# A three-stage decoder layer on one core: mask bound, weight splits and the self-attention tail moved, and the output projection placed ahead of probabilities-by-values

## The reference, cut to what matters

```python
def _L0_attn_ref(x, Wq, bq, Wk, bk, Wv, bv, Wo, bo):
    q = (x @ Wq.T + bq).reshape(b, l, h, hd).transpose(0, 2, 1, 3)
    k, v = ...
    scores = jnp.einsum('bhqd,bhkd->bhqk', q, k) / math.sqrt(hd)
    att = jax.nn.softmax(jnp.where(causal, scores, -jnp.inf), axis=-1)
    return jnp.einsum('bhqk,bhkd->bhqd', att, v)... @ Wo.T + bo
def _L0_xattn_ref(query, key, value, mask, wq, wk, wv, wo):
    q, k = _rope(q), _rope(k)
    scores = jnp.einsum('bhgqd,bhkd->bhgqk', qg, k) / scale
    masked = jnp.where(mask[:, None, None].astype(bool), scores, -1000000000.0)
    return (softmax(masked) @ v) @ wo
x = _layernorm(x + _L0_attn_ref(x, ...))
x = _layernorm(x + _L0_xattn_ref(x, ctx_4096, ctx_4096, mask, ...))
x = _layernorm(x + _L0_ffn_ref(x, ...))
```

## Time and profile before

| what | before |
|---|---|
| runs | 1770.31, 1770.8 (median), 1776.01 us |
| the profiled execution's own time | 1773.97 us |
| its span, first to last instruction | 1772.2 us |
| mean granted TensorE clock | 0.982 of full speed |
| PE busy | 1695.6 us (96% of the span) |
| DVE, POOL, ACT busy | 1267.5, 964.8, 919.0 us |
| self-attention | from 0 to about 302 us |
| cross-attention | from about 303 us |

### The profile page before, as it was taken

The page is one execution under the profiler, slowest core; times in us unless marked ns, Lnnn a source line. Parts: engine busy times, 40 slices in busy tenths (PEclk is TensorE's granted clock), DMA queues, the critical chain, the costliest instruction groups (busy, mean ns, idle before and its releaser), DMA issues. The chain is left out here.

```text
span 1772.2 us, 39039 instructions
## 1 busy us (share of the span) xinstructions
PE 1695.6 (96%) x15461; PEld 968.1 (55%) x15461; DVE 1267.5 (72%) x2048; ACT 919.0 (52%) x1518; POOL 964.8 (54%) x875
## 2 busy tenths in 40 slices
PE   6899998699999999999999999999889999999997
PEld 4666665365555555555555555555555555455553
DVE  5777776678888888888888888888786444344445
ACT  5776764555546564646464555455742333333334
POOL 5556672745645454646464646464743555455545
PEclk9999999899999999999999999999988999999999
DMA  4522312311312222214131222121166778887658
GB/s 147 146 65 47 85 48 36 117 37 58 110 62 83 83 68 89 97 42 149 37 108 61 72 72 96 37 104 40 61 226 198 153 151 222 221 208 153 115 100 300
DMA packets 88897, 190.68 MB, mean 108 GB/s; under 512 B 14800, under 2 KB 33744, under 8 KB 86672
## 3 DMA queue, kind: packets, MB, share of 16 engines
q1 hardware_dynamic: 65232, 130.72, 22.1%
q0 software_dynamic: 22912, 57.32, 15.8%
q10 hardware_dynamic: 576, 0.14, 0.0%
HBM read 124.95 MB, written 63.21 MB: 106 GB/s over the span
## 5 line engine op out<-in xcount | busy, mean ns | idle before, releaser
L1112 POOL TENSOR_TENSOR xa_sc<-xa_sc,xa_rs 128x1024 f32<-128x1024 f32 x32 | 60.9, 1903 | 374.4 <-DVE xa_rs L1360 374.4
L1099 POOL TENSOR_TENSOR xa_xs<-xa_xs,sn 128x512 f32<-128x512 f32 x160 | 234.1, 1463 | 45.7 <-ACT xa_xs L1153 45.7
L288 PE MATMUL bank<-xhl,front_h 128*128 128x512 f16 x640 | 245.4, 383 | 10.9 <-DVE front_l L648 9.7
L289 PE MATMUL bank<-xhl,front_h 128*128 128x512 f16 x640 | 245.2, 383 | 0.0
L290 PE MATMUL bank<-xhl,front_l 128*128 128x512 f16 x640 | 245.0, 383 | 0.0
L1104 POOL TENSOR_TENSOR xa_rr<-xa_x,xa_xs 128x512 f32<-128x512 f32 x160 | 232.9, 1456 | 12.7 <-DVE xa_x L1260 0.2
L2006 POOL DMA_INDIRECT scratch_y<-raw_front,moe_to x79 | 125.3, 1586 | 149.1 <-DVE mo_zl L2060 126.8
L288 PE MATMUL bank<-out_h,xa_oh 128*128 128x512 f16 x512 | 194.1, 379 | 10.3 <-DVE xa_ol L1242 6.7
L290 PE MATMUL bank<-out_h,xa_ol 128*128 128x512 f16 x512 | 194.0, 379 | 0.0
L289 PE MATMUL bank<-out_l,xa_oh 128*128 128x512 f16 x512 | 194.0, 379 | 0.0
L1152 ACT ACTIVATE xa_xs<-bank 64x512 f32<-64x512 f32 x160 | 95.1, 595 | 140.7 <-PE bank L290 126.5
(11 more groups left out here) (318 smaller groups left out, 4665.5 us busy)
## 6 DMA issues: line engine op xcount, KB each, us to landing
xa_rawc<-in_ew SPq DMA_DIRECT2D x32, 768.0 KB, 5.5
moe_ring<-scratch_w SPq DMA_DIRECT2D x16, 1536.0 KB
scratch_w<-xa_chunk_h SPq DMA_DIRECT2D x32, 384.0 KB, 2.3
scratch_w<-xa_chunk_l SPq DMA_DIRECT2D x32, 384.0 KB, 3.3
raw_front<-in_xwq SPq DMA_DIRECT2D x8, 1024.0 KB, 7.8
raw_out<-in_xwo SPq DMA_DIRECT2D x8, 1024.0 KB, 5.3
scratch_y<-acc SPq DMA_DIRECT2D x6, 1024.0 KB, 5.8
acc<-in_x POOLq DMA_DIRECT2D x4, 1024.0 KB, 7.7
```

The lines of the kernel that those rows point to most:

```text
L288: pe.matmul(out_ap, ah, bh, start=start and m == 0, stop=False)
L289: pe.matmul(out_ap, ah, bl, start=False, stop=False)
L1099: PO.mark(pool.tensor_tensor(xr, xr, sn[:, :].rearrange("p (a s) -> p a s", a=1) .to_broadcast([P, QT // S, S]), ALU.mult), f"sm{r}", st)
L1112: PO.mark(pool.tensor_tensor(s4, s4, rs[:, :, :].rearrange("p h (t a) -> p (h t) a", a=1) .to_broadcast([P, 16, S]), ALU.mult), "nm", st)
```

## The change

Six edits, in the program's order.

1. First step of self-attention: the weights arrive, are split and are used in the order keys, queries, values (before: keys, values, queries). On ACT `qh` comes between the two masked key copies and the values' copy comes after them; DVE's `ql` and PE's scores wait for the second key copy by a semaphore of their own.
2. `front_high(2)`, `front_high(3)` and the output weights' high half move on ACT from before `qh` to the start of steps 1, 2 and 3. Their low halves stay where they are on DVE.
3. In each step with an output tile, PE does w ahead of pv.
4. The last block: `next_keys` stands between `pt0` and `pt1`, two thirds of `next_values` ahead of pv and a third behind it; on DVE `ol` comes after the last of the four subtractions.
5. The bound: its tile outlives the stages and shares its bytes with `late_h` and the keys `kk`. SP loads it once the last step's q and ko are done, and POOL converts it after its last self-attention step. Both leave the first cross-attention step.
6. The first group's output weights of cross-attention are split in the first step: ACT in one piece between its first and second copies, DVE in four pieces (`out_lo`).

```diff
@@ self_attention, ACT
-                    for n in (0, 2, 1):
+                    for n in range(3):
                         act.wait_ge(s_w0[n], 16)
...
                     def step(n):
                         st, tile, turned = step_of(n), normed_tile(n), turned_tile(n)
+                        if n in (1, 2):
+                            front_high(n + 1)
+                        if n == 3:
+                            act.wait_ge(s_ro, 16)
+                            act.activation(out_h[:, :], raw_out[:, :], ACT.Copy, scale=WS).then_inc(s_wo_a, 1)
                         if n > 1:
                             back_o(st, n - 2)
...
                         else:
                             front_high(1)
+                            keys_of(st, 0)
+                            act.wait_ge(s_first_q, 1)
+                            queries_of(st)
+                            keys_of(st, 1).then_inc(s_first_qh, 1)
+                            values_out(st)
-                        if n in (1, 2):
-                            front_high(n + 1)
-                        if n == 3:
-                            act.wait_ge(s_ro, 16)
-                            act.activation(out_h[:, :], raw_out[:, :], ACT.Copy, scale=WS).then_inc(s_wo_a, 1)
@@ self_attention, PE
-                        if n:
-                            back_pv(st, ("w",) if tile is None else ())
                         if tile is not None:
...
                             output(tile, home["w"], "w", st)
+                        if n:
+                            back_pv(st)
...
-                    back_p(done, (0, 1))
-                    back_p(done, (2, 3))
+                    back_p(done, (0,))
                     pe.wait_ge(s_cq, 2)
                     pe.wait_ge(s_upper, 1)
                     pe.wait_ge(DV.sem, DV.value("sb2", done))
                     next_keys(pe)
+                    back_p(done, (1,))
+                    back_p(done, (2, 3))
+                    pe.wait_ge(DV.sem, DV.value("sb3", done))
+                    next_values(pe, (0, 1))
                     back_pv(done)
-                    pe.wait_ge(DV.sem, DV.value("sb3", done))
-                    next_values(pe)
+                    next_values(pe, (2,))
@@ self_attention, SP and POOL, at their ends
+                    last = step_of(STEPS - 1)
+                    sp.wait_ge(PE.sem, PE.value("q", last))
+                    sp.wait_ge(AC.sem, AC.value("ko", last))
+                    for h in range(2):
+                        sp.dma_start(bound[64 * h:64 * h + 64, :, :], maskf.rearrange("b q k -> q b k")).then_inc(s_mask, 16)
...
+                    pool.wait_ge(s_mask, 32)
+                    limit = bound[:, :, :].rearrange("p b k -> p (b k)")
+                    chain(pool.tensor_scalar(limit, limit, 0.0, 0.0, ALU.is_equal, ALU.is_equal))
+                    chain(pool.tensor_scalar(limit, limit, BIG, -1e9 * float(HD2) ** 0.5, ALU.mult, ALU.add))
@@ cross_attention, POOL, ACT and DVE
-                            if first and (q, r) == (0, 2):
-                                mask_bound(pool)
...
                         copies(st, 0)
-                        copies(st, 1)
-                        if q == 1:
+                        if alone:
+                            act.wait_ge(s_ro, 16)
+                            act.activation(wo_h[:, :, :], raw_o[:, :, :], ACT.Copy, scale=WS).then_inc(s_first_out, 1)
+                        copies(st, 1, ("woh",) if first and q == 1 else ())
+                        if q == 1 and i:
...
+                    def out_lo(dve, h):
+                        dve.scalar_tensor_tensor(wo_l[:, h, :], raw_o[:, h, :], WS, wo_h[:, h, :], ALU.mult, ALU.subtract)
```

116 lines of the change are left out of this document (65 added, 51 removed).

## The result

| what | before | after |
|---|---|---|
| median (lowest to highest), 9 runs each | 1771.29 us (1770.13 to 1776.01) | 1760.18 us (1755.46 to 1765.12) |
| ratio, 95% interval | | 0.9936 [0.992, 0.9951] |
| profiled execution, span | 1773.97, 1772.2 us | 1761.15, 1759.4 us |
| granted clock | 0.982 | 0.986 |
| PE busy | 1695.6 us | 1689.2 us |

The change is faster by 11 us, 0.6%. Forecast were 24 us and 1746.8 us, with a range of 1740 to 1757: it is faster, as forecast, but by 13 us less, and 1760.2 us lies above the range. All times in this text are those of fast runs; beside e9 to e11 one execution of the kernel before took 9922 us, and it is left out of their ratios.

The account below looks back on a forecast made before the run. PE, busy 96% of the span, was taken as the bound, its few waits also lowering the clock. 7.6 + 3.3 + 1.4 - 0.5 + 0.7 + 8.0 + 3.5 = 24.0 us off 1770.8 gives 1746.8 us; range 1740 to 1757.

Parts of the forecast that it names:

- edit 1, first step: First self-attention step: scores start near 20.95 us instead of 22.35, a gain of 1.4 us.
- edit 2 and the clock behind its waits: Self-attention steps 1 to 3: shorter waits before the scores give 7.6 us, higher clock behind them 3.3 us.
- edit 3: Eleven self-attention steps: w ahead of pv gains nothing itself and delays `oT`; 0.5 us lost, bounds 0 and 3.
- edit 5: First cross-attention step: without POOL's two passes, second-block scores start 8.0 us earlier, bounds 5 and 10.
- edit 6, less 1.5 in the way: Second cross-attention step gains 3.5 us; 1.5 us was taken off edit 5 for `out_l` pieces and possible lower clock.
- The clock: Sign of being right, in self-attention: granted clock at 0.97 or more from 40 to 80 us.
- The second score block: Sign of being right, first cross-attention step: some 19 us behind the stage's first product instead of 27.2.
- not a full blocking: First cross-attention step: rows beside POOL showed only a longer `out_l`, 0.84 against 0.57 us a piece.
- rival B: First cross-attention step: `out_l` pieces and POOL block each other at the port; 5 us go, 1752 us; chance 12%.
- D: Rival: gains are hidden by something later, such as a cross-attention chain; under 5.3 us left, 1769 us; chance 4%.
- C: Rival: in 11 self-attention steps late pv delays everything behind it; 29.7 us lost, 1776 us; chance 2%.
- A: Rival: clock still falls from 40 to 80 us, cross-attention rotations only 5 us earlier; 1754 us; chance 20%.

Follow-up runs that it names:

- e9: The changed kernel with 64 small matrix products added at PE's very start, where it waits for the first weights: 1767.1 us, ratio to before 0.9966.
- e11: e1 with only the transfer of cross-attention's output weights issued later, behind w of step 5: 1754.1 us, ratio to before 0.9897.
- e2: The kernel before with edit 3 (w ahead of pv) as its only edit: 1776.9 us, ratio to before 1.0023.
- e6: e1 with the weight splits of steps 1 to 3 put back behind the key copies (edit 2 undone): 1763.0 us, ratio to before 0.9945.
- e1: The changed kernel with edit 3 undone, so pv is ahead of w again: 1753.0 us, ratio to before 0.9893.
- e7: e1 with POOL's two passes over the bound back in the first cross-attention step, the mask still loaded early: 1763.2 us, ratio to before 0.9947.
- e8: e1 with the first group's output weights split in the second cross-attention step again (edit 6 undone): 1757.0 us, ratio to before 0.9912.
- e4: e1 with SP issuing cross-attention's weights only behind w of step 5, not in steps 2 and 3: 1754.0 us, ratio to before 0.9897.
- e12: e1 with 64 small matrix products added at PE's start: 1755.5 us, ratio to before 0.9898.
- e10: The changed kernel with 32 small matrix products added at PE's very start: 1764.2 us, ratio to before 0.9949.
- e5: e1 with six more long products of no use between pv and the scores in steps 1 to 4: 1762.3 us, ratio to before 0.9945.

## Why the prediction was wrong, step by step

| term | predicted | measured |
|---|---|---|
| edit 1, first step | 1.4 | 1.9 against before; 0.6 against e2, which has the old first step too |
| edit 2 and the clock behind its waits | 7.6 + 3.3 | 6.0 at the last tiles (e6); 9.2 by the ratios |
| edit 3 | -0.5, bounds 0 and 3 of loss | -3.4 (e2), -6.8 (e1, of which 2.6 from the stop of step 3) |
| edit 5 | 8.0, of which 0.9 the mask's transfer | 6.9 for the passes alone (e7) |
| edit 6, less 1.5 in the way | 2.0 net | 1.6 to 1.9 (e8) |

Edit 4 was not tried alone. The measured terms need not add up to 12.5, since each was taken beside other edits.

**The step that failed is the sentence on edit 3, "this can gain nothing by itself in a step where PE never waits", with its sum.** I priced the new order only by what other engines then deliver late. That price was right: the wait for `oT` is 0.3 us. But PE also needs its own instructions, and the long w products between pv and the scores were the time in which they came: 3.4 us lost with edit 3 alone (e2), about 4 us in the tile steps of the changed kernel. The upper bound of the loss, 3 us, was too small for the same reason, since no row on "issue" had been used for it.

**The same omission is in edit 2.** "Nearly all of the 2.51 us goes" is true of the wait for `ql`. What took over was not `ql`, as I wrote, but the fetch: 7.4 us of "issue" without the waits and 3.0 us with them. So in self-attention 6.0 us were gained and not 10.9. I had the evidence: "issue" 3.3 us in three stops inside the scores, in steps without any of these waits.

Without edit 3 the forecast would have been 24.5 us, and e1 gained 19.0 us by its ratio. At the last tiles e1 is 9.9 us ahead of before, where 13.0 were forecast, and cross-attention adds 9.5 instead of 11.5.

**The clock.** Right from 40 to 60 us (1.00), wrong from 60 to 80 (0.83): the low clock of step 3 follows a stop of 3.18 us as it followed the waits of before; behind e1's stop of 1.33 us the clock stayed full.

**Cross-attention.** The bound's passes are where they were forecast, and `ptl` beside them is untouched. POOL's rows and DVE's mean over all 64 `ptl` rows of self-attention, beside the earlier trace rows:

```profile
276.42 7.11 POOL L534 TENSOR_SCALAR bound<-bound 128x2048 f32<-128x2048 f32 x1 [3.06 <-DMA bound<-in_maskf]
283.62 1.90 POOL L535 TENSOR_SCALAR bound<-bound 128x2048 f32<-128x2048 f32 x1
...
L683 DVE TENSOR_TENSOR sa_ptl<-bank,sa_pth 128x512 f16<-128x512 f32 x64 | 41.2, 682 | 4.8 <-ACT sa_pth L563 4.8
```

682 ns as before. The second score block came 21.1 us behind the stage's first product, not 19. In this first step DVE's and POOL's rows held each other:

```profile
307.68 1.80 POOL L1123 TENSOR_TENSOR xa_xs<-xa_xs,sn 128x512 f32<-128x512 f32 x1
308.42 1.61 DVE L1290 TENSOR_TENSOR xa_rql<-xa_rr,xa_rqh 128x512 f16<-128x512 f32 x1
311.30 1.27 POOL L1123 TENSOR_TENSOR xa_xs<-xa_xs,sn 128x512 f32<-128x512 f32 x1
311.86 1.25 DVE L1294 SCALAR_TENSOR_TENSOR out_l<-raw_out,out_h 128x512 f16<-128x512 f32 x1
312.64 1.59 POOL L1128 TENSOR_TENSOR xa_rr<-xa_x,xa_xs 128x512 f32<-128x512 f32 x1
313.04 1.74 DVE L1290 TENSOR_TENSOR xa_rql<-xa_rr,xa_rqh 128x512 f16<-128x512 f32 x1
```

Each of these DVE rows ends 0.54 or 0.55 us after the POOL row beside which it started (309.48 and 310.03, 312.57 and 313.11, 314.23 and 314.78 us). Over the whole kernel 96 of the 128 `rql` rows start while a POOL row runs, and 94 of them end 0.55 us after it; the 31 that have no POOL row beside them take 0.68 us. The Trainium skill ("SBUF — State Buffer", section "Who interferes with whom") has the later of two such instructions blocked until the first ends, and these rows agree. So the prediction's "not a full blocking" was a wrong reading. What keeps the price small is that the POOL rows are short and nearly over: it is a share of rival B (I had 5 us for it; 2 us of the rotations are missing here). One kind of row does not fit: beside the pass of 7.11 us, held DVE rows ended 5.07 us after its start, 2.0 us before its end (`xa_rql` of 4.88 us before, an `out_l` piece of 4.34 us in e7).

**Rivals.** The prediction's D, the gain lost later, is out: 12.4 us at 400 us and 12.8 at the end. C had the right suspect, edit 3, and the wrong mechanism. A said "thinner cover" and 1754 us; it named no fetch. None of the four had this cause, and the chance of one that was not on the list was given nothing.

The version that beats both is e1: all edits but the third, 1753.0 us. (e4, e11 and e12, built on it, cannot be told from it.)

## What to carry to other kernels

Take an "issue" wait inside a run of short products seriously. Look whether its places are a fixed number of instructions apart. If they are, count the products of a block and the time that they take before moving anything. Do not put two stretches of short products back to back: long ones between them covered the fetch wherever the borders lay, except where a load filled the DMA engines, and idle time that you remove may have been covering it too. Where such stops exist, a few instructions added anywhere ahead can move a border into a load: 32 and 64 small products made cross-attention end 6 and 8 us later here. So judge a small edit against a padded copy as well.

## What the runs showed of the hardware that was not expected

- PE fetches its program in blocks of 256 instructions: 1280 instructions from stop to stop, packets of 16,384 bytes, 0.9 to 1.6 us long at the stops. PE goes on 1.2 to 1.7 us after the packet has landed, in all 85 stops. A block of short products that PE works through in 1.7 us ends in a stop of 1.2 us.
- The packets share the DMA engines with the data: beside loads PE stopped for 3.2 us (step 3), 4.8 us (e10, step 3), 4.3 us (e10) and 5.55 us (e9), the last two beside the mask's transfer of small packets (2120 of them in e9's window).
- Long products do not protect in every case: 3.7 us (e5) and 4.1 us (e12) of stop stood inside the keys' projection.
- A wait can be put down to the wrong engine: e10's 4.32 us "DVE sa_mx" is such a fetch.
- A DVE row with two SBUF inputs that starts beside a POOL row of 1.3 to 1.8 us ends 0.55 us after it (94 of 96 rows); alone it takes 0.68 us.
